# Query projections issued half a block earlier, and split waits before the router logits, in a fused attention and expert-routing kernel

## What is computed

```python
q, k, v = split(H @ W_qkv.T + b_qkv);  q, k = elu(q) + 1, elu(k) + 1
kv, k1 = einsum('hnd,hnv->hdv', k, v), k.sum(over tokens)
out = (q @ kv) / clip(q . k1, 1e-6)
out = layernorm(out @ W_proj.T + b_proj) * gamma + beta + H
x = layernorm(H + out)                      # the rows that the experts read
Sm = softmax(x @ Wr + br)                   # logits of 8 experts per token
G, idx = top_k(Sm.T, 512)                   # every expert's best 512 tokens
y[idx] += G * (silu(x[idx] @ W_up + b_up) @ W_down + b_down)
result = layernorm(x + y)
```

## Time and profile before

| | us |
|---|---|
| median of 3 runs | 446.09 |
| the runs | 445.10, 446.09, 449.98 |
| the profiled execution | 448.76 |
| its span, from first to last instruction | 446.9 |
| its mean granted TensorE clock | 0.911 |

### The profile page before, as it was taken

How to read it: one execution, slowest core, us unless ns; L and a number is a source line. 1 busy time by engine, 2 the same in 40 slices (tenths; PEclk the granted TensorE clock), 3 DMA queues, 4 the chain that set the end, 5 groups by cost and what they waited for, 6 DMA issues and landing times.

```text
span 446.9 us, 5591 instructions
## 1 busy us (share of the span) xinstructions
PE 363.9 (81%) x1631; PEld 241.4 (54%) x1631; DVE 238.9 (53%) x882; ACT 148.5 (33%) x350; POOL 165.7 (37%) x250
## 2 busy tenths in 40 slices
PE   4889999878998892110499999999999999999930
PEld 3678886445776661000356656475665647465520
DVE  2765564675898887888753755613030121048540
ACT  1433332334676884430022030311203030237700
POOL 0300043000458786000342243534424263554853
PEclk9999999899999997555569999989999999999985
DMA  8934544500023455900110261614524163589641
GB/s 264 298 126 141 188 141 142 172 1 1 24 96 119 154 177 189 12 1 1 50 48 25 65 133 50 110 29 105 113 79 57 50 110 111 100 253 365 236 162 47
DMA packets 49631, 50.75 MB, mean 114 GB/s; under 512 B 12138, under 2 KB 42563, under 8 KB 49603
## 3 DMA queue, kind: packets, MB, share of 16 engines
q1 hardware_dynamic: 43650, 40.32, 30.5%
q0 software_dynamic: 5952, 10.10, 11.3%
HBM read 32.97 MB, written 17.43 MB: 113 GB/s over the span
## 4 chain that ended last, share of the span: by engine, by line
PE 61%; DVE 16%; POOL 9%; issue 6%; DMA 3%; ACT 1%; POOLq 0%; SPq 0%; DVEq 0%; ACTq 0%
PE ps L801 16%; PE ps L772 15%; PE ps L621 6%; PE ps L613 6%; PE ps L597 5%; PE ps L746 4%; POOL rstd L1383 3%; PE ps L684 3%; PE ps L697 3%; DVE qexp L1009 2%; DMA out<-h_all 1%; PE ps L759 1%; DMA heads<-ysum,idx 1%; POOL ysum L1436 1%; DVE ht_all L1125 1%
## 5 line engine op out<-in xcount | busy, mean ns | idle before, releaser
L801 PE MATMUL ps<-wdn_s,ht_all 128*128 128x256 f32 (+1 forms) x384 | 96.9, 399 | 0.0
L772 PE MATMUL ps<-xgt,wup_s 128*128 128x512 f32 (+1 forms) x192 | 88.4, 613 | 0.0
L801 PEld LDWEIGHTS ps<-wdn_s,ht_all 128*128 128x128 f32 (+1 forms) x384 | 68.8, 192 | 25.5 <-issue 18.4
L1331 ACT ACTIVATE ht_all<-ps,bup_s 128x512 f32<-128x512 f32 (+1 forms) x48 | 33.0, 687 | 126.3 <-PE ps L772 126.3
L1429 POOL DMA_INDIRECT xg<-table,idx x32 | 32.4, 1012 | 93.3 <-DVE idx L1132 55.5
L772 PEld LDWEIGHTS ps<-xgt,wup_s 128*128 128x128 f32 (+1 forms) x192 | 33.6, 183 | 47.7 <-issue 47.7
L1436 POOL DMA_INDIRECT ysum<-yb,idx x24 | 40.6, 1690 | 48.1 <-DVE yb L1163 42.6
L1163 DVE TENSOR_SCALAR yb<-ps,gate 128x256 f32<-128x256 f32 x24 | 11.6, 484 | 57.3 <-PE ps L801 57.3
L597 PE MATMUL ps<-wqkv_s,heads 128*128 128x264 f32 x128 | 32.8, 403 | 7.3 <-DMA heads<-xt 5.5
L697 PE MATMUL ps<-wp_s,turned 128*128 128x264 f32 x128 | 33.7, 385 | 0.0
L597 PEld LDWEIGHTS ps<-wqkv_s,heads 128*128 128x128 f32 x128 | 25.3, 199 | 12.1 <-issue 7.7
(11 more groups left out here) (189 smaller groups left out, 529.4 us busy)
## 6 DMA issues: line engine op xcount, KB each, us to landing
wdn_s<-wdn SPq DMA_DIRECT2D x8, 640.0 KB
heads<-xt SPq DMA_DIRECT2D x8, 512.0 KB, 3.9
h_all<-x SPq DMA_DIRECT2D x8, 512.0 KB, 5.0
ht_all<-xtq SPq DMA_DIRECT2D x8, 512.0 KB, 3.6
table<-x SPq DMA_DIRECT2D x32, 128.0 KB, 1.7
ysum<-x SPq DMA_DIRECT2D x32, 128.0 KB, 1.8
h_all<-ysum SPq DMA_DIRECT2D x8, 512.0 KB, 8.8
out<-h_all SPq DMA_DIRECT2D x8, 512.0 KB, 5.5
```

The lines of the kernel that those rows point to most:

```text
L772: mm = pe.matmul(ps[0:width, f % 2, :], wup_s[:, c, f * P:f * P + width], xgt[:, c, :], start=(c == 0), stop=(c == C - 1))
L801: mm = pe.matmul(ps[:, bank, 0:D], mid[0:rows_, f, j * P:(j + 1) * P], wdn_s[0:rows_, f, :], start=(f == 0), stop=(f == FT - 1))
L1331: act.activation(mid[0:width, f, :], ps[0:width, f % 2, :], ACT.Silu, bias=bup_s[0:width, e // GS, f:f + 1]).then_inc(s_mid, 1)
```

## The change

Two edits. First, TensorE issues the halves of the queries elsewhere: the first half of block 1 before the stage's first attention tile, then in each block `n` half 1 of block `n + 1` behind tile 0 and half 0 of block `n + 2` behind tile 2. Their number and their waits (the PSUM bank read, the input landed) stay. No other engine's order changes. Second, in `logit_rows` the wait for `rstd` up to `end + 2`, which stood before the first instruction, becomes one for `end` before the second and one for `end + 2` before the sixth.

```diff
@@ logit_rows
             eng.wait_ge(s_sq, end)
-            eng.wait_ge(s_rs, end + 2)
             eng.tensor_tensor(at, z8[:, first:end, :], row(kr[:, 1, :]), ALU.subtract).then_inc(s_logit, 1)
             eng.wait_ge(s_logit, done + 1)
+            eng.wait_ge(s_rs, end)
             eng.tensor_tensor(at, at, column(rstd[:, first + 1:end + 1, 0]), ALU.mult).then_inc(s_logit, 1)
...
             eng.wait_ge(s_logit, done + 5)
+            eng.wait_ge(s_rs, end + 2)
             eng.tensor_tensor(at, at, column(rstd[:, first + 3:end + 3, 1]), ALU.mult).then_inc(s_logit, 1)
@@ block.tensor
+            def next_queries(n, m):
+
+                pe.wait_ge(s_qread, C * (n - 1) + (m + 1))
+                if m == 0:
+                    pe.wait_ge(s_ht, 16 * n + 16)
+                queries(n, m)
+
@@ block.tensor, tokens(n, t)
-                if prefetches(n) and t < C:
-
-                    pe.wait_ge(s_qread, C * n + (t + 1))
-                    if t == 0:
-                        pe.wait_ge(s_ht, 16 * n + 32)
-                    queries(n + 1, t)
+                if prefetches(n) and t == 0:
+                    next_queries(n + 1, 1)
+                if prefetches(n + 1) and t == C:
+                    next_queries(n + 2, 0)
...
+            next_queries(1, 0)
             pe.wait_ge(s_kv, 1)
             tile_steps(tokens)
```

## The result

The changed kernel takes 440.98 us (median of 7 runs, 439.07 to 442.52), the kernel before in the same series 448.94 (7 runs, 444.92 to 449.98). The ratio estimated from the runs is 0.9857, with a 95% interval of 0.9821 to 0.9893: 1.4% faster, or 6.4 us.

What follows compares the result with a forecast made beforehand. It took three limits in turn: TensorE's wait for `qt`, TensorE itself, then GpSimd's chain before the logits. Terms 4.5 - 0.34 + 1.05 = 5.2 us off the median of 446.09 gave 440.9, range 438.8 to 444.3.

Steps and rivals of the forecast that it cites:

- The waits of blocks 1 to 3: TensorE's waits for `qt` at the starts of blocks 2 to 4 and their restarts go: 4.5 us gained.
- The block length of 5.3: Blocks 1 to 3: TensorE's own work, four attention tiles and two query halves, sets the block at 5.3 us.
- the cover: Blocks 1 to 3: `qt` reaches TensorE at 4.95 us, 0.35 us before its own work of 5.3 ends.
- rival (a): Middle stage: VectorE takes over as limit and loses its slack in blocks 4 to 6; 2.6 us go, 443.5; chance 0.14.
- The 0.34 at the end: Blocks 4 to 7: last half issued a tile earlier, so VectorE sets seven end tiles instead of six; 0.34 us lost.
- The opening: Block 0: the early first half is moved, not added; net 0 of TensorE's time, the wait of about 2.06 us stays.
- The logits: VectorE's logit rows: its 1.16 us wait for GpSimd's last `rstd` goes; less the added waits' price, 1.05 us gained.
- The cover at the sixth instruction: Logits: the sixth instruction comes at 176.26, after `rstd` at 175.45, so the wait is covered by 0.8 us.
- the 0.05 each: Logits: two instructions get a second wait, priced at 0.05 us for each, bounds 0 and 0.2.
- The clock: Opening: the low clock stays with the wait of about 2.06 us, costing 1.69 us as before.
- (b): Opening: the clock does not fall in the changed kernel; 1.7 us more gained, 439.2; chance 0.12.
- (c): Opening: the median of before has no clock fall and the changed kernel has one; 442.6; chance 0.10.

Runs made afterwards that it cites:

- e1_queries: Only the moved query halves, the logits' wait put back as before, against the changed kernel: 441.98 us, ratio to the kernel before 0.9896.
- e6_cover: Both query halves later, behind tiles 2 and 3, against the changed kernel with `prepare()` in front of the tiles: 447.97 us, ratio to before 1.0027.
- e4_prepare_old: `prepare()` in front of the tiles, queries and waits as before, against the kernel before: 443.79 us, ratio 0.9930.
- e5_opening: The opening's two halves back behind tiles 0 and 1 of block 0, later ones moved, against the changed kernel: 438.58 us, ratio to before 0.9808.
- e2_waits: Only the split wait before the logits, queries as before, against the kernel before: 447.43 us, ratio 1.0000.
- e0_after: The changed kernel run once more, nothing altered, in a later series: 441.56 us, ratio to the kernel before 0.9881.
- e7_adjacent: Only half 0 later, behind tile 3, against the changed kernel with `prepare()` in front of the tiles: 441.52 us, ratio to before 0.9844.

## Why the prediction was right

**The waits of blocks 1 to 3.** The sum had 4.5 - 0.34 = 4.16 for the queries; e1_queries measured 4.27. The block length of 5.3 came out as 5.35, and 5.52 at block 4, where the two waits more stayed, as was allowed for. `qt` was in time, and no wait came back; but the cover was about 0.1, not 0.35. In the changed kernel block 2 starts at 90.03 and block 3 at 95.45 (the second tile of the two that TensorE runs in a row there). ScalarE ends 4.18 behind the start of block 2, as the text has it (4.2). VectorE is later than that:

```profile
92.94 0.17 DVE L954 TENSOR_SCALAR den<-ps 128x16 f32<-128x16 f32 x1 [0.36 <-PE ps L692]
...
94.60 0.68 DVE L891 SCALAR_TENSOR_TENSOR qt<-qexp,qrel 128x512 f32<-128x512 f32 x1
```

It works through tiles 1 and 2 one behind the other and begins with `qt` 4.57 behind the start, where the text had 4.0, as if VectorE were free when the third tile came. With the 0.75 to TensorE that is 95.35, 0.1 ahead of the next block. The same gap in the reckoning, three tiles taken at 0.46 each, is what e6_cover ran into.

The sign of rival (a) did not come: the first wait for `zg` or `heads` on TensorE is at 132 us, behind the last half of the queries, and up to 160 us there are 2.4 us of them, where before had 2.9.

**The 0.34 at the end.** The rows give both terms. From the start of block 1 to the first half of the queries in block 4, TensorE took 105.38 + 0.70 - 82.88 - 1.69 = 21.51 us before, the fall taken off, and takes 101.59 - 84.64 = 16.95 now: 4.56 less, for the 4.5. The stage keeps 4.27 of that (e1_queries), so some 0.3 is lost behind it, for the 0.34. It is not lost in the way that the sum has it, though. These are VectorE's `us` lines next to GpSimd's own eight logit rows, before and in e1_queries:

```profile
140.22 0.49 DVE L939 SCALAR_TENSOR_TENSOR us<-zg,rstd,h_all 128x256 f32<-128x256 f32 x1 [0.99 <-POOL rstd L1383]
```

```profile
133.74 0.49 DVE L945 SCALAR_TENSOR_TENSOR us<-zg,rstd,h_all 128x256 f32<-128x256 f32 x1 [0.21 <-POOL rstd L1389]
```

Counted from the first mark and without the fall, e1_queries is 3.48 ahead of before at the `us` line in front of these (137.04 and 131.33), and 4.25 at these. So about 1.1 was lost up to there, not 0.34, and 0.77 of it came back out of a wait for GpSimd that stood there before anyway. That this term came out right is luck: the text let VectorE and GpSimd move there as they stood.

**The opening.** "Net 0" is right against before: the wait of 2.05 stayed, 1.7 later. But the text took the wait for the price of prepare alone. In the old order it was not: without prepare in its way 1.22 of the 2.06 stayed (e4_prepare_old). And e5_opening shows that the early half is a cost of its own, 1.65, which the half of block 2 in the old wait could pay back.

**The logits.** 1.05 predicted, 1.07 measured twice. The cover at the sixth instruction is 0.54, not 0.8, because GpSimd's last `rstd` ends 1.32 behind the first logit line (168.58 to 169.90), where I had 1.03 (174.42 to 175.45). The two waits more cost next to nothing where they stand, for the 0.05 each: from the first logit line to `mx` it takes 2.76 with them (168.58 to 171.34) and 2.74 without (175.58 to 178.32). What 1.07 lacks of 1.16 lies in front of the logits: VectorE's last two `us` lines start 1.35 apart in e2_waits and 1.22 in before, for a reason that the rows do not show.

**The clock.** I had the fall bound to the wait of about 2 us, and in both kernels. It was there in both profiles, but not for that reason in the changed one, and e0_after has the wait without the fall. The rivals (b) and (c), a fall in one kernel and not in the other, are both what single executions do: the same program took 102.48 with a fall and 100.80 without one. That agrees with the rule on the free-running watch which the prediction cites from the Trainium skill (TensorE: Matmul & The Clock Gate, Part 1).

**The total.** 440.9 was said and 440.98 measured, but that closeness is partly luck. The step in the stage, 5.34 against 5.2, is the prediction's own. The level of before is not: three runs put its median at 446.09, and the later series at 448.94, 446.82, 446.59 and 448.48. From the 448.94 of the changed kernel's own series the same 5.2 would have given 443.7, 2.8 too much. The runs' interval of 0.9821 to 0.9893 is 4.8 to 8.0 us, and 5.3 lies in it.

## What to carry to other kernels

Where an engine's queue is in order and the kernel waits once in every block, look for work of a later block that could stand ahead of the link that is late. Here it cost nothing where it only filled the wait (4.27 us won), and the profile's chain gave the new block length in advance (5.3, and 5.35 measured). How much cover is left has to be worked out for each engine's whole queue in the new order, not for one tile. Where such work is put decides as much as that it is early: between two tiles that share banks it also covered the time in which a bank is read out, so spread it evenly (uneven, it cost 3.1 us here, and late as well, 10.0). And a fixed piece of work that another engine does inside the first blocks belonged in front of them here, under something long that was there anyway (2.2 us).

## What was not expected of the hardware

The fall of the clock in the opening has no single cause that the rows show. In before it fell at 84.0 and in e2_waits at 81.0, some 1.1 and 0.4 us behind a wait of 2.06; in e0_after and e1_queries the same wait was there and it did not fall. In the changed kernel (74.2), e4_prepare_old (75.0) and e7_adjacent (75.2) it fell with no wait in front. There TensorE's rows are busy without a break, with the short matmuls of the weights' folding; but e0_after has the same rows and no fall there, so these are no cause by themselves either. It fell from 2.4 to 1.2 GHz each time, in five of the twelve profiled executions. The two falls whose price was worked out cost 1.69 (before) and 1.68 us (the changed kernel). An execution without one is therefore no sign of a better order.
